# Set-up of a two-layer gated transformer kernel: gate scalars on GpSimd's queue, x in four transfers behind the small tables, tanh later, one weight copy ahead of the root

## The reference, cut to what matters

```
x = x + tanh(g_xattn[0]) * L0_xattn(layernorm(x), ctx, ctx, boxes, ...)   # 16 heads of 64, box-relation gate
x = x + tanh(g_ffn[0])   * L0_ffn(layernorm(x), ...)                      # ternary weights
x = x + tanh(g_xattn[1]) * L1_xattn(layernorm(x), ctx, ...)
x = x + tanh(g_ffn[1])   * L1_ffn(layernorm(x), ...)                      # 8 experts, top 2
```

## Time and profile before

| | |
|---|---|
| median of 3 runs | 1144.31 us (1140.92 to 1145.85) |
| profiled execution, its own time | 1143.62 us |
| its span in the trace | 1141.6 us |
| busy: PE / DVE / ACT / POOL | 949.0 / 817.9 / 684.2 / 710.1 us |
| first PE instruction | 33.12 us after the start |
| first `separable` instruction on POOL | 23.39 us |
| first copy of half an expert started | 68.92 us |

### The profile page before, as it was taken

One profiled execution on the slowest core, in us unless ns is written; L12 is line 12 of the kernel. 1 busy time (PEld: TensorE's weight loads), 2 busy tenths in 40 slices (PEclk: granted clock), 3 DMA queues, 4 the chain that ended last, 5 costly groups with the idle time before them and its releaser, 6 DMA issues.

```text
span 1141.6 us, 32938 instructions
## 1 busy us (share of the span) xinstructions
PE 949.0 (83%) x12178; PEld 777.1 (68%) x12178; DVE 817.9 (72%) x1957; ACT 684.2 (60%) x1342; POOL 710.1 (62%) x811
## 2 busy tenths in 40 slices
PE   0448999999999985589876569982899999999995
PEld 0336777777777764455544458861899999999995
DVE  3997888788877876677877689956566666666663
ACT  2457888888888883066543468854354454545452
POOL 2988888875777653035453279965466666666662
PEclk9889999999999997689988789985899999999998
DMA  9277776787767656411000100003553225832251
GB/s 280 76 188 150 135 150 153 157 175 171 146 154 159 137 109 167 143 51 41 1 1 1 40 2 21 21 21 100 165 152 103 33 40 168 268 91 32 32 143 14
DMA packets 52117, 119.65 MB, mean 105 GB/s; under 512 B 7616, under 2 KB 30144, under 8 KB 51632
## 3 DMA queue, kind: packets, MB, share of 16 engines
q0 software_dynamic: 14144, 35.48, 21.6%
q1 hardware_dynamic: 35520, 80.71, 21.1%
q10 hardware_dynamic: 2352, 2.10, 0.6%
HBM read 212.54 MB, written 37.85 MB: 219 GB/s over the span
## 4 chain that ended last, share of the span: by engine, by line
PE 53%; DVE 14%; POOL 11%; ACT 9%; DMA 7%; issue 5%; SPq 0%; ACTq 0%; POOLq 0%; DVEq 0%
PE bank L2168 17%; PE bank L2182 8%; POOL PT L565 6%; PE bank L1827 5%; PE bank L1730 3%; PE bank L1929 3%; DVE nmx L1209 2%; PE bank L1968 2%; PE bank L1807 2%; ACT EX L1424 2%; PE bank L1941 2%; PE bank L1769 2%; ACT L1393 1%; PE bank L1762 1%; DMA gates<-in_g_ffn 1%
## 5 line engine op out<-in xcount | busy, mean ns | idle before, releaser
L1664 ACT ACTIVATE yg<-bank,bms 128x128 f32<-128x128 f32 x312 | 106.9, 363 | 113.2 <-PE bank L2168 103.3
L1327 DVE TENSOR_TENSOR hm<-hf,hm 128x256 f16<-128x256 f32 x156 | 66.7, 427 | 90.8 <-ACT hm L1671 87.0
L1322 DVE SCALAR_TENSOR_TENSOR hf<-bank,bms,yg 128x128 f32<-128x128 f32 x312 | 98.8, 347 | 32.1 <-ACT yg L1664 29.4
L2168 PE MATMUL bank<-xT,wm_even 128*128 128x128 f16 x1920 | 116.2, 221 | 1.9 <-DVE xT L1334 1.0
L709 POOL DMA_INDIRECT out_x<-ys,sidx x39 | 62.7, 1608 | 83.2 <-DVE ys L1341 83.2
L2168 PEld LDWEIGHTS bank<-xT,wm_even 128*128 128x128 f16 x1920 | 111.5, 99 | 3.5 <-DVE xT L1334 1.4
L2168 PE MATMUL bank<-xT,wm_odd 128*128 128x128 f16 x1824 | 109.9, 220 | 2.0 <-DMA wm_odd<-expert_weights 2.0
L2168 PEld LDWEIGHTS bank<-xT,wm_odd 128*128 128x128 f16 x1824 | 105.5, 99 | 3.1 <-issue 2.2
L1671 ACT ACTIVATE hm<-hf 128x256 f16<-128x256 f32 x156 | 64.7, 415 | 63.9 <-DVE hf L1322 62.8
L565 POOL TENSOR_TENSOR PT<-PT 128x512 f16<-128x512 f32 x64 | 72.3, 1157 | 41.7 <-ACT PT L1450 41.6
L551 POOL TENSOR_TENSOR q<-qt,q 128x512 f16<-128x512 f32 x64 | 79.9, 1276 | 1.0 <-ACT q L1437 0.9
(11 more groups left out here) (309 smaller groups left out, 2660.2 us busy)
## 6 DMA issues: line engine op xcount, KB each, us to landing
wm_even<-expert_weights SPq DMA_DIRECT2D x60, 1024.0 KB
wm_odd<-expert_weights SPq DMA_DIRECT2D x57, 1024.0 KB
expert_weights<-in_wcat POOLq DMA_DIRECT2D x16, 768.0 KB, 7.8
wsp<-expert_weights SPq DMA_DIRECT2D x16, 768.0 KB, 4.4
wsp<-in_wcat POOLq DMA_DIRECT2D x16, 768.0 KB, 10.6
expert_weights<-wsp SPq DMA_DIRECT2D x16, 768.0 KB, 3.3
Lst<-gate_tables SPq DMA_DIRECT2D x48, 68.0 KB, 5.8
gate_tables<-Lw SPq DMA_DIRECT2D x6, 512.0 KB, 4.6
```

The source lines that it names most:

```text
L1322: v.scalar_tensor_tensor(hf[:, (c // 2) % 2, c % 2, :], bank[c % 4][:, MT:2 * MT], bms[:, par, FC + c:FC + c + 1], yg[:, c % 4, :], ALU.ad ...
L1327: v.tensor_tensor(hm16[:, par, 1, c - 1:c + 1, :], hf[:, q % 2, :, :], hm16[:, par, 0, c - 1:c + 1, :], ALU.subtract).then_inc(m_hl, 1)
L1664: s.activation(yg[:, c % 4, :], bank[c % 4][:, 0:MT], ACT.Gelu, bias=bms[:, par, c:c + 1]).then_inc(m_g, 1)
L2168: ins = t.matmul(bank[c % 4][:, w * MT:(w + 1) * MT], wm16[par][:, wp, col:col + P], xT16[:, par, xp * KD + kk, :], start=(n == 0), stop=( ...
```

## The change

The gate scalars are started by POOL's queue rather than ACT's. ACT starts only a quarter of x (4 batches) at once, then waits for the four small tables and starts the other three quarters; DVE's statistics wait for the first quarter, and then for all three others together. The tanh moves behind the third weight copy, the first weight copy ahead of the root. Four small memsets on DVE move to the front. On POOL `split_qk(0, 0)` moves ahead of the last two of the eight `separable`.

```diff
-        s_x, s_c, s_cs, s_cw = sem("x_loaded"), sem("consts_loaded"), ...
+        s_c, s_cs, s_cw = sem("consts_loaded"), sem("sizes_loaded"), sem("boxes_loaded")
...
+        a_ld = sem("x_rest_and_l1_weights_loaded")
+        s_x = (sem("x_loaded"), a_ld)
...
+            gp.dma_start(gates[:, 0:2], a["g_xattn"].partition_broadcast(P)).then_inc(s_c, 16)
+            gp.dma_start(gates[:, 2:4], a["g_ffn"].partition_broadcast(P)).then_inc(s_c, 16)
             gp.wait_ge(s_wha, 2)
             gp.wait_ge(s_cs, 16 * 4)
...
-            split_qk(0, 0)
+            for j in range(NJ):
+                if j == NJ - 2:
+                    split_qk(0, 0)
+                separable(0, j, pc.n + 5 * j)
+                if j == 3:
+                    split_ctx(0, 0)
+                    split_ctx(1, 1)
             split_v(0, 0)
...
-            dv.wait_ge(s_x, 16)
...
                 for b in range(B):
+                    if b % 4 == 0:
+                        dv.wait_ge(s_x[b > 0], 48 if b else 16)
                     ins = v.bn_stats(bst[:, b, :], X[:, b, :])
...
-            ac.dma_start(X[:, :, :], a["x"].rearrange("b n d -> n b d")).then_inc(s_x, 16)
-            ac.dma_start(gates[:, 0:2], a["g_xattn"].partition_broadcast(P)).then_inc(s_c, 16)
-            ac.dma_start(gates[:, 2:4], a["g_ffn"].partition_broadcast(P)).then_inc(s_c, 16)
-            ac.wait_ge(s_c, 32)
-            s.activation(tg[:, :], gates[:, :], ACT.Tanh).then_inc(s_tg, 1)
+            def load_x(q):
+                ac.dma_start(X[:, 4 * q:4 * q + 4, :], a["x"][4 * q:4 * q + 4, :, :].rearrange("b n d -> n b d")).then_inc(s_x[q > 0], 16)
+
+            load_x(0)
+            ac.wait_ge(s_cs, 16 * 4)
+            for q in range(1, 4):
+                load_x(q)
             ac.wait_ge(s_whv, 1)
             s.activation(wha[:, :, :], wha[:, :, :], ACT.Ln).then_inc(s_wha, 1)
             ac.wait_ge(s_whv, 2)
             s.activation(wht[:, :, :, :], wht[:, :, :, :], ACT.Sin, scale=TWO_PI).then_inc(s_wha, 1)
-            ac.wait_ge(s_var, 1)
-            s.activation(rstd_t[:, 1, :], rstd_t[:, 0, :], ACT.Sqrt).then_inc(s_sqrt, 1)
...
             weight_high(0)
+            ac.wait_ge(s_var, 1)
+            s.activation(rstd_t[:, 1, :], rstd_t[:, 0, :], ACT.Sqrt).then_inc(s_sqrt, 1)
             weight_high(1)
...
             weight_high(2)
+            ac.wait_ge(s_c, 32)
+            s.activation(tg[:, :], gates[:, :], ACT.Tanh).then_inc(s_tg, 1)
...
-            ac.wait_ge(a_ld, 80)
+            ac.wait_ge(a_ld, 128)
```

More of the change, by code:

```diff
@@ L280, in build @@
         s_tg = sem("tanh_ready")
-        s_x, s_c, s_cs, s_cw = sem("x_loaded"), sem("consts_loaded"), sem("sizes_loaded"), sem("boxes_loaded")
+        s_c, s_cs, s_cw = sem("consts_loaded"), sem("sizes_loaded"), sem("boxes_loaded")
         s_w, s_whi = [sem(f"{n}_weight_staged") for n in "qkv"], sem("weight_split_hi")
@@ L325, in build @@
         m_o, m_y = sem("expert_out_full"), sem("expert_out_taken")
-        a_ld, a_w, a_wl = (sem("l1_" + n) for n in ("weights_loaded", "weights_high", "weights_low"))
+        a_ld = sem("x_rest_and_l1_weights_loaded")
+        s_x = (sem("x_loaded"), a_ld)
+        a_w, a_wl = (sem("l1_" + n) for n in ("weights_high", "weights_low"))
         a_qf, a_kf, a_raw, a_red, a_v = (sem("l1_" + n) for n in ("q_full", "kv_full", "raw_copied", "squares_summed", "v_copied"))
@@ L764, in step @@
                 dv.wait_ge(s_pv, vc.up(ins))
+            for par in range(2):
+                v.memset(vv16[:, par, 0, :, DK:DK + 1], 1.0)
+                ins = v.memset(vv16[:, par, 1, :, DK:DK + 1], 0.0)
+            step(ins)
             dv.wait_ge(s_cs, 16 * 4)
@@ L832, in weight_low @@
                 v.scalar_tensor_tensor(wqkv16[:, j, 1, :, :], wst[j], WSC, wqkv16[:, j, 0, :, :], ALU.mult, ALU.subtract).then_inc(s_wlo, 1)
[L834 to L837, removed]
             def key_centres(b0, b1):
```

## The result

| | before | changed |
|---|---|---|
| median of the runs | 1144.55 us (4 runs) | 1164.9 us (1161.12 to 1165.66, 4 runs) |
| ratio, 95% interval | | 1.0176 (1.0144 to 1.0209) |
| profiled execution's time / span | 1143.62 / 1141.6 us | 1161.12 / 1158.9 us |

The changed kernel is slower by 20.3 us. The direction was forecast, the size was not: 6.2 us had been forecast, and the range ended at 1153.5. Five more runs of the changed kernel, made later beside the kernel before, gave 1.0175 (1.0144 to 1.0207). The changed kernel's profile is of the fastest of its four runs, so the two profiled executions are only 17.5 us apart.

The account below looks back on a forecast made before the run. The start of the half-expert copy, hanging on x, DVE and q, was taken to bound the kernel. It moves from 68.92 to 75.3, +6.4 us: 1150.0 from the profiled execution, 1150.7 from the median, written as 1150.5; range 1139.5 to 1153.5.

Parts of the forecast that it names:

- What bounds the kernel, and that x would be late: Set-up: the start of the half-expert copy moves POOL and ACT; x lands at 31.3 us rather than 16.3.
- The rival with x ahead of the broadcasts: Loading x: the 413 packets left pass before or within the first `cm`, landing 22.8, total 1142.2 us; chance 0.16.
- the one with shares by bytes: Loading x: x gets half of the bytes or the tail is shorter; landing 18.0, total 1137.4 us; chance 0.12.
- the rule of the Trainium skill on whole packets of 9 to 17 descriptors: DMA engines: one ring's whole packet drains before the next ring's turn; x would be through about 8.5 us sooner.
- I take 6.8, and 1.6 us from issue to first data, so the other 1536 packets begin at 8.4: Loading x: small tables land at 6.8 us, and x's last three quarters start moving at 8.4.
- the rule of the queues: DMA: SP's and ACT's queues alternate packet by packet, whatever a packet's size.
- the count ahead of the wide rows: Loading x: 1123 x packets pass in step with SP's 1123 before the broadcasts, leaving 413 at 17.4 us.
- the sentence that the broadcasts bracket the end: Loading x: starting x a microsecond sooner or later shifts its landing by under one.
- From x to the copy: x normalised at 39.2 us, first q copy at 59.9, half-expert copy 15.4 later at 75.3, four low halves taking 4.5.
- 82.0 ... so 1.5 us of slack stay, less if stores and copy share the engines: SP: table stores and reads end at 82.0 us, before the half-expert copy lands at 83.5.
- The rival with SP's queue: SP: stores, reads and half-expert copy delay each other by 3 to 4 us, adding 2 to 3, about 1153; chance 0.10.
- The sum: Half-expert copy starts at 75.3 us against 68.92, +6.4 us, bounds +3.9 to +8.9.

Follow-up runs that it names:

- gates_only: Kernel before, with only the gate scalars issued by POOL's queue and their tanh behind the third weight copy; ratio to before 0.9982 (0.9953 to 1.0011).
- x_first_order_back: Changed kernel, with all quarters of x issued at once and the low halves of q and k behind all eight separables; ratio to before 0.9976.
- early_copy: Changed kernel, with POOL issuing the first two half-expert copies ahead of the low halves of q and k; ratio to before 1.0111.
- x_first: Changed kernel, with all four quarters of x issued at once, ahead of the wait for the small tables; ratio to before 1.0042.
- order_only: Kernel before, with only the low halves of q and k moved ahead of separables 6 and 7 on POOL; ratio to before 1.0049.

## Why the prediction was right in direction and wrong in size

*What bounds the kernel, and that x would be late:* right for a later start, which is this case. The chain ran from x through DVE and q to the copy, POOL stood still twice, and the early start of POOL (forecast 14 to 16, measured 16.23) was lost in the wait for the context. For an earlier start it was not right that the copy moves ACT: `gates_only` started it 5.9 us sooner and gained 2.1 at ACT's exponentials, `x_first_order_back` 6.6 us sooner for 2.7 us of time. The prices of the faster rivals, one us of time for each us of the copy, were too high. The rival with x ahead of the broadcasts, the one with shares by bytes and the rule of the Trainium skill on whole packets of 9 to 17 descriptors ("DMA: Bandwidth & Descriptors", queues, rings and completion order) all asked for a landing before 25 us; 38.0, and 36 packets against 34 beside 8 KB rows, speak against them.

*"I take 6.8, and 1.6 us from issue to first data, so the other 1536 packets begin at 8.4":* this step failed. The small tables landed at 9.01 as before, and ACT's next packets did not follow 1.6 but 3.7 us behind the issue at 9.03. No run shows the 1.6: the first quarter had its first packets 1.2 us behind its issue, and the last packet of x passed 0.7 us ahead of the landing. Between 8.5 and 12.7 SP moved 780 packets, and ACT none:

```profile
DMA packets 783, 1.71 MB, mean 408 GB/s; under 512 B 54, under 2 KB 409, under 8 KB 783
q1 hardware_dynamic: 780, 1.71, 105.5%
```

Some 350 of them are the context's rows of 512 bytes, two thirds of all, small packets beside which x would have moved cheaply. At 16.5 us, when the wide rows begin, 451 packets of x's second batch had passed, not 1123, so about 1085 were left rather than 413. From there to 28 us the alternation held, 401 packets beside SP's 400, and the rest went behind that, beside the last wide rows and the biases, until 37.3:

```profile
q1 hardware_dynamic: 400, 1.96, 85.6%
q10 hardware_dynamic: 401, 0.39, 19.4%
```

So the rule of the queues was right and the count ahead of the wide rows wrong. Landing 38.0 against 31.3: 6.7 us of the error. With it falls the sentence that the broadcasts bracket the end and a microsecond at the start shifts it by under one: in `early_copy` x joined 1.5 us sooner and landed 4.6 sooner.

Nor was it x that kept the small tables: the first quarter was through by 4.5 us. From 4.5 to 6.5 us all queues together moved little (in the kernel before 0.75 MB):

```profile
DMA packets 245, 0.22 MB, mean 112 GB/s; under 512 B 115, under 2 KB 203, under 8 KB 245
```

In this stretch POOL's queue brings the gate scalars. In `x_first`, where most of their packets pass from 6.5 to 8.5 us, the low rate is there (0.28 MB). That the scalars cause it was not tried.

*From x to the copy:* right. Landing to x normalised 7.5 us against 7.9, on to the first q copy 20.5 against 20.7, on to the copy of half an expert 16.5 against 15.4. The last has an error of its own: the four low halves took 6.37 us beside DVE, not 4.5.

*"82.0 ... so 1.5 us of slack stay, less if stores and copy share the engines":* this step failed too. I carried the 6.2 us from the earlier trace rows into a place where the stores no longer run alone. They share with the copies, packet by packet, and the table store takes 13.1 us instead of about 3; SP's reads begin 16.5 us after the last separable (80.3 to 96.8), not 6.2. The rival with SP's queue had the place and the mechanism, and a chance of 0.10 at 2 to 3 us; it was worth 7.2 (20.8 at POOL's restart less 13.6 at the copy) and was no alternative but an addition. `order_only` shows it without the late x, `early_copy` shows what it shares with.

*The sum:* on top of the 6.4 that had been forecast come 6.7 for x, 0.5 for the stretches behind it and 7.2 for SP. That makes 20.8 at POOL's restart; 20.3 are measured in time.

Left open: why ACT's second batch of transfers begins 3.6 to 3.7 us behind its issue, and why the small tables landed at 7.56 in one profile and at 9.01, 9.34 and 9.63 in three others with the same front part (x at 33.4, and at 38.0 to 38.5). Neither was tried. Open too is what decides how long TensorE's clock stays low after such a pause.

## What to carry to other kernels

A transfer that is issued second on another queue isn't merely behind: in all these runs it moved one of its rows for each row of the other queue, so narrow rows beside wide ones crawl. Put the narrow one first, keep wide rows back until it has landed, or cut them. When an instruction stream is reordered, price each transfer that changes its company, small stores on a waited-for semaphore above all, by what it costs beside that company and not by what it cost alone. A head start on an engine is worth only what its next wait leaves of it.

## What the runs showed of the hardware that was not expected

- Two hardware queues alternate packet for packet even at 8 KB against 1 KB (36 against 34 in a microsecond), and the software queue and SP's queue do so too: 49 against 43 packets in 88 to 90 us of the changed kernel, 0.30 MB against 0.18.

```profile
q0 software_dynamic: 49, 0.30, 76.7%
q1 hardware_dynamic: 43, 0.18, 23.2%
```

- DVE and POOL slow each other down when they work side by side: POOL's four low halves took 4.49 us in the kernel before and 6.37 in the changed one, and eight box distances 5.76 and 8.03 us before, 2.14 (at 97.47) when POOL stood still in the changed kernel.
- After nearly equal pauses of TensorE (4.95, 4.96 and 4.95 us) the granted clock stayed at the 1.2 GHz level for some 4 us in the kernel before and in `x_first_order_back`, and for some 9 us in `gates_only`. Two executions of the changed kernel differ in the same way, some 4 us and some 9 behind the restart. That goes with about 1 us at the milestone (1.1 between the two executions), so a single profile can't settle differences of that size.
- A small store on a semaphore that is waited for costs what its company costs: the tables' 32 KB landed 13.1 us after their issue beside the copies of half an expert, and SP's wait for them was 4.2 us without.
